# Order of the maxima and the transposed-block copies on VectorE in eight self-attention passes

## What is computed

```
x = x + tanh(g_xattn[i]) * xattn_i(layernorm(x), ctx)
x = x + tanh(g_ffn[i])   * ffn_i(layernorm(x))
```

```
att = q k^T * scale;  att = where(causal, att, -inf)
y   = softmax(att) v  + softmax(qc kc^T * scale) vc
```

```
a = softmax(q k^T * D**-0.5);  a = a * (key > query);  o = a v
```

## Time and profile before

| what | us |
|---|---|
| median of three runs | 3064.89 |
| profiled execution | 3065.05 |
| span of the profiled execution | 3063.3 |
| TensorE matmul busy | 2480.4 |
| VectorE busy | 1309.0 |
| ScalarE busy | 889.6 |
| GpSimd busy | 690.2 |

### The profile page before, as it was taken

The page is one execution under the profiler, slowest core; times in us unless marked ns, Lnnn a source line. Parts: engine busy times, 40 slices in busy tenths (PEclk is TensorE's granted clock), DMA queues, the critical chain, the costliest instruction groups (busy, mean ns, idle before and its releaser), DMA issues.

```text
span 3063.3 us, 32462 instructions
## 1 busy us (share of the span) xinstructions
PE 2480.4 (81%) x11538; PEld 1646.6 (54%) x11538; DVE 1309.0 (43%) x2768; ACT 889.6 (29%) x1970; POOL 690.2 (23%) x767
## 2 busy tenths in 40 slices
PE   4888978879487619997489988989988667999995
PEld 2444644546346517775144555544555435888873
DVE  5555245553544421112475453465443542333324
ACT  0635235542242102221164422364422110111110
POOL 3421231222100040002301032110032054222236
PEclk7999989999698659998699999999988678999998
DMA  9000000000002032221000000000000033555533
GB/s 358 16 1 1 1 1 1 1 1 1 14 0 111 0 123 92 90 93 47 26 1 1 1 1 1 0 1 1 1 1 1 1 134 129 194 197 204 195 133 116
DMA packets 65152, 175.15 MB, mean 57 GB/s; under 512 B 6656, under 2 KB 45696, under 8 KB 56832
## 3 DMA queue, kind: packets, MB, share of 16 engines
q0 software_dynamic: 21504, 96.49, 9.1%
q1 hardware_dynamic: 43536, 77.18, 7.1%
HBM read 123.18 MB, written 50.46 MB: 57 GB/s over the span
## 4 chain that ended last, share of the span: by engine, by line
PE 62%; DVE 13%; issue 11%; POOL 9%; ACT 3%; DMA 1%; SPq 0%; DVEq 0%; POOLq 0%; ACTq 0%
PE PS L1943 8%; PE PS L553 6%; PE PS L953 5%; PE PS L944 5%; PE PS L1728 5%; PE PS L1742 5%; PE PS L1955 4%; PE PS L583 4%; PE PS L494 3%; PE PS L903 3%; PE PS L533 2%; POOL slots L2043 2%; POOL arena L2057 2%; PE PS L743 2%; DVE arena L657 2%
## 5 line engine op out<-in xcount | busy, mean ns | idle before, releaser
L614 ACT ACTIVATE arena<-PS,arena 128x512 f32<-128x512 f32 (+3 forms) x512 | 305.4, 605 | 215.4 <-DVE arena L657 201.7
L553 PE MATMUL PS<-arena 64*128 64x512 f32 (+3 forms) x1024 | 296.5, 566 | 53.4 <-ACT arena L614 42.6
L657 DVE TENSOR_REDUCE arena<-PS 128x1 f32<-128x512 f32 (+3 forms) x512 | 272.5, 581 | 33.5 <-PE PS L559 24.9
L274 POOL TENSOR_TENSOR arena<-arena 128x4 f32<-128x4 f32 x53 | 55.6, 1050 | 938.1 <-DVE arena L285 375.4
L1943 PE MATMUL PS<-arena 128*128 128x256 f32 (+1 forms) x1152 | 260.3, 382 | 0.9 <-DVE arena L1979 0.9
L1943 PEld LDWEIGHTS PS<-arena 128*128 128x128 f32 (+1 forms) x1152 | 210.1, 182 | 42.1 <-issue 1.3
L837 POOL TENSOR_TENSOR arena<-arena 128x512 f32<-128x512 f32 x144 | 118.2, 825 | 434.5 <-ACT arena L810 427.0
L553 PEld LDWEIGHTS PS<-arena 64*128 64x128 f32 x1024 | 102.4, 186 | 168.3 <-ACT arena L614 115.6
L583 PE MATMUL PS<-arena 128*128 128x128 f32 x1280 | 178.9, 289 | 15.5 <-ACT arena L614 15.5
L583 PEld LDWEIGHTS PS<-arena 128*128 128x128 f32 x1280 | 147.2, 148 | 68.9 <-ACT arena L614 50.1
L944 PE MATMUL PS<-arena 128*128 128x512 f32 x384 | 168.3, 594 | 3.1 <-ACT arena L961 3.1
(11 more groups left out here) (333 smaller groups left out, 3972.1 us busy)
## 6 DMA issues: line engine op xcount, KB each, us to landing
arena<-e SPq DMA_DIRECT2D x8, 2048.0 KB, 8.5
arena<-slots SPq DMA_DIRECT2D x56, 256.0 KB, 3.4
yslots<-arena POOLq DMA_DIRECT2D x56, 256.0 KB, 2.6
slots<-zeros SPq DMA_DIRECT2D x1, 12288.0 KB, 40.5
slots<-zeros SPq DMA_DIRECT2D x1, 5120.0 KB, 35.9
arena<-w3a SPq DMA_DIRECT2D x1, 4106.0 KB, 13.1
arena<-w3b SPq DMA_DIRECT2D x1, 3593.0 KB, 21.1
arena<-slots SPq DMA_DIRECT2D x8, 384.0 KB, 8.8
```

Source lines behind the costliest of these rows:

```text
L553: ins = nc.tensor.matmul(PS[:, hh, 0:w], q[:, t * P:(t + 1) * P], k[:, 0:w], start=True, stop=not cfg["causal"])
L614: nc.scalar.activation(PRB[m % 6][:, 0:w], PS[:, hh, 0:w], ACT.Exp, bias=nmax[:, m:m + 1], accum_out=rsum[:, col:col + 1]).then_inc(s["pro ...
L657: nc.vector.tensor_reduce(nmax[:, m:m + 1], PS[:, hh, 0:w], AX, ALU.max, negate=True).then_inc(s["nmax"], 1)
```

## The change

In each step VectorE takes all four maxima first, then the product of `shared_out` where there is one, and then all its transposed blocks of the step before. Before, the product and the first transposed block came between maxima 1 and 2. ScalarE's and TensorE's lists are as they were: ScalarE still copies its first odd block between exponentials 1 and 2.

```diff
@@ -682,17 +682,14 @@
                 if n < NSTEPS:
                     top(n, 0)
                     top(n, 1)
+                    top(n, 2)
+                    top(n, 3)
                 if n >= 3:
                     shared_out(n - 3)
-                if n >= 1:
-                    turn(n - 1, 0, 1)
-                if n < NSTEPS:
-                    top(n, 2)
-                    top(n, 3)
                 if n == 0:
                     dve_project(v, s, it, cfg, "v")
                 if n >= 1:
-                    turn(n - 1, 1, 3)
+                    turn(n - 1, 0, 4)
                     if between is not None:
                         between(n)
                     out_ = at_step[n - 1][1]
```

## The result

The changed kernel takes 3022.45 us (median of 4 runs, 3020.33 to 3023.16), the kernel before 3067.22 (median of 4 runs, 3061.54 to 3070.28). The ratio is 0.9854, with a 95% interval of 0.9839 to 0.9868: 45 us faster, where 22 were forecast from the first three runs' median.

A forecast was written before the change was run, and what follows sets the result against it. Order and hand-overs bound the kernel: TensorE's waits in the loop of maximum, exponential, next score, transposes. Layer 0's 7.8 us plus layer 3's 15.3 make 23; 3065 less 23 is 3042, given as 3043, range 3031 to 3056.

The forecast's parts named there:

- The score that waited 1.26 us at 1582.33: Layer 3, score matmul idling on exponential 2: its wait would fall from 1.26 to about 0.5 us.
- decoy: Layer 0, 2.59 us idle before exponential 2 after a one-block step: looks like the prize, costed at 0.
- The bank's stall: Layer 3 four-block transposes: fourth block waits for block 0's later copy; taken as 0.1 us, bounds 0 to 1.1.
- The slower rival: Block 0's copy delays the fourth block 1.1 us at 12 layer 3 transitions: 13 us lost, 3078; chance 0.06.
- The product's place: Product of line 678, put behind the maxima: covered by 2.4 us in layer 3, at most 2.8 us in layer 0.
- "hidden" rival: TensorE bounds each group and exponential 2's gain is waited for elsewhere: 3060 to 3065 us; chance 0.11.
- exponential 2 is held only by ScalarE's copy: Layer 3 two-block step: with maxima moved ahead, exponential 2 starts at 1580.75 for 1581.50, 0.75 us earlier.
- layer 0, per group: Exponential 2 starts about 0.23 and 0.13 us earlier in two steps, carried on: 0.36 us per four steps.
- layer 0, added in a pass's first group: No value matmuls stand in between, so exponential 2's earlier start reaches the next score: 0.5 us taken.
- layer 3, three-block step, added: Exponential 2 gains 0.22 us more from its idle time, beyond the 0.75 carried over: 0.97 in all.
- layer 3, per period: What is left of the 0.97 us for the value matmul at 1592.81 after the four-block transposes' stall: 0.85 us.
- the clock rival: Shorter gaps remove three or four low-clock stretches of some 3.5 us, beyond the forecast gain: 3031 us; chance 0.10.

The follow-up runs named there:

- four_old: Changed kernel, but in layer 3's four-block step block 0's copy stands before maxima 2 and 3 again; 3024.05 us, ratio 0.9854.
- product_first: Changed kernel, but the product of line 678 goes back between maxima 1 and 2; 3025.72 us, ratio 0.9849.
- act_late_but_four: Changed kernel, with ScalarE's odd-block copies behind all exponentials of a step, except the first copy in four-block steps; 3008.12 us, ratio 0.9816.

## Why the prediction fell short

Its reading of the loop was right in these points:

- The score that waited 1.26 us at 1582.33 waits 0.30 (0.5 forecast).
- The step after a one-block step was a decoy, as said: its exponential 2 starts 1.47 us after the scores (118.25 to 119.72) for 2.46 before (139.60 to 142.06), and nothing follows from it. I had said over 1 us earlier; it then waits for the transposes that free its buffer.
- The bank's stall was put at 0.1 us within 0 to 1.1, and is 0.13 in the rows and 0.10 in `four_old`. The slower rival needed 1.9 and is dead.
- The product's place costs nothing (`product_first`).
- The gain lies inside the passes, and the "hidden" rival would have been wrong by 45 us: TensorE works 89% of the windows, and the gain still came out of its waits. The rule of the Trainium skill, Perfetto Trace Analysis, section "Identifying the Most-Contended Engine", taken as the prediction takes it, as a forecast, ends in the same place, and the measured ratio of 0.9854 goes against that reading. The rule itself only names the engine, here TensorE, and it was TensorE's waits that became shorter; no run here goes against it. Nor does the trace bear out the page's sentence on matmul busy time, as the prediction has it: that the missing 11% are waits tells of the room in the loop, not of how good a measure busy time is.

**The step that failed** is "exponential 2 is held only by ScalarE's copy, 1580.05 + 0.60", and likewise 114.64 to 114.70 in layer 0: the time at which exponential 2 is let go. I added the copy's duration where the next ScalarE instruction starts 0.49 us after the copy's start. That is 0.11 us, and 0.03 to 0.10 of hand-over that isn't there, twice per group, and it carries through to the next score. A row of the kernel before had it already, after a step's second copy, where nothing else is waited for (0.49 us from start to start):

```profile
137.96 0.59 ACT L629 ACTIVATE arena<-PS 128x512 f32<-128x512 f32 x1
138.45 0.47 ACT L614 ACTIVATE arena<-PS,arena 128x256 f32<-128x256 f32 x1
```

In the three-block step "only" was wrong as well: the end of the transposes holds exponential 2 at the same moment (`act_late_but_four`). The terms, forecast and measured in full clock:

| term | forecast | measured |
|---|---|---|
| layer 0, per group | 0.36 | 0.65 |
| layer 0, added in a pass's first group | 0.5 | 0.7 |
| layer 0, a pass | 1.9 | 3.3 |
| layer 3, two-block step | 0.75 | 0.95 |
| layer 3, three-block step, added | 0.22 | 0.39 |
| layer 3, per period | 0.85 | 1.22 |
| layer 3, a pass | 3.8 | 5.3 |
| eight passes | 23 | 34.5 |

**The second term that failed** is the clock, which the sum put at nothing. The passes together gave 46.3 us. 34.5 is the order, and the remaining 12 are the clock (2.6 in layer 0, 9 in layer 3). That is the size that the clock rival had, but I gave it a chance of 0.10 as an alternative, where it was an addition: the lower level went away together with the standing stretches that the order shortened, and should have been summed, at least in the range. The two misses are of one size, 11.5 us of order and 12 of clock: either alone would have left the time near the lower end of the stated range, 3031. That standing still brings the lower level is shown where dummy work filled the standing stretches, and argued for the rest.

The 12 is a difference, and for the first and third passes of layer 3 it leans on the yardstick of the other two; a clean pass of that kind in the old order was not seen. 93.01 us at 0.98 clock is its upper bound; less the 1.5 us that 0.98 cost in the fourth pass it would be 91.5, an estimate, and 5.5 above the 86.0 of the new order. The split between order and clock in layer 3 is thus shown for two passes and inferred for two.

## What to carry to other kernels

Price a queued instruction by the distance between its start and its successor's in a stretch without waits, not by its duration: in a loop through several engines that difference comes back at each hand-over. Then name the next limit behind the one removed. Here that was ScalarE's copy, worth 13 us in the clean passes once the maxima were early and nothing before, and right behind it, in the three-block step at the same moment, the transposes. Where two limits end together, removing one of them shows nothing: measure from the start of the work that both depend on. Where TensorE stands still in the old order, count the clock into the sum and the range, not only among the rivals.

## What the runs showed of the hardware

A ScalarE copy of 128x512 from PSUM lasts 0.60 us, but the exponential behind it starts 0.49 us after the copy's start. The traces have this in 107.20 to 107.69 and 1563.86 to 1564.36 (changed kernel), 1568.27 to 1568.76 (`product_first`) and 137.96 to 138.45 (kernel before).

Twelve transposes of useless work in each of two waits made a pass shorter (89.38 us for 93.83 with the granted clock back from 0.93 to 1.00), where the Trainium skill, TensorE: Matmul & The Clock Gate, section "HAM oscillation — how this bites in real kernels", has its case with waits for DMA between tiles. Here a wait of 1.59 us on ScalarE stood before the lower level. With the wait filled to 0.28 us that stretch was gone, and two of the four passes of layer 3 were in full clock, the other two at 0.98. In the kernel's whole time the dummies could not be told from nothing (0.9992).
